# Pre-norm attention and binary feed-forward layer on one core: a transfer queue in another order, masks laid by small matmuls, normalisations with a tensor as third operand

## The chip, the cores and the metric

The kernel runs on one core of a Trainium2 chip. Its program is written out for each engine: PE (TensorE, matrix multiplication into PSUM), DVE (VectorE), ACT (ScalarE), POOL (GpSimd) and SP (SyncE, which here only issues DMA transfers, in order). The engines meet in semaphores. The metric is the time of one launch on the device in microseconds (us).

## The reference

```python
# x: (8, 1024, 256); 16 heads of 16; window 128
def attn(x):
    q = (x @ Wq.T + bq).reshape(B, S, 16, 16)      # k and v alike
    scores = einsum('bqhd,bkhd->bhqk', q, k) * 0.25
    mask = (j <= i) & (j >= i - 128)
    attn = softmax(where(mask, scores, -10000.)) + 1e-9
    return einsum('bhqk,bkhd->bqhd', attn, v).reshape(B, S, 256) @ Wo.T + bo
x = x + attn(layernorm(x))
x = x + einsum('bsi,oi->bso', layernorm(x), sign(weight))
```

## The kernel before

Each of the 8 sequences is cut into 8 tiles of 128 rows, and two tiles make a pair. The program is a software pipeline of slots, one for each of the 64 tiles and four more. In a slot each engine works on stages of different tiles. `parts(b, t)` says which: for slot t, `nm` (turn the negative row maxima of tile t+2 and store them), `mx` (the rough scores of tile t+3 for its row maxima), `pv` (probabilities times values, tile t-1), `xr` (load x of tile t-2 again), `op` (output projection and first residual of tile t-3), `ff` (second layer and store of tile t-4). Stages of a pair run in every other slot: `tqv` (transpose, q and v projections) and `load` (load x) in odd slots; `k` (k projection) and `ln` (first layer norm, two tiles) in even ones. "Odd" and "even" below are the slot's number; slot numbers run on over the sequences, eight to each.

What the change and the prediction touch:

- **The SP queue.** `slot` in the SP program runs through the stages in written order. In an odd slot: the stored maxima (`stack_nmax`, L296), `load_x` (L242), `stack_q` (L252 and L262: it waits for `q_16`, which ACT makes near the end of that slot, then issues 2 + 6 transfers), `load_xr` (L303), and the store of the result (L323). In an even slot: `stack_nmax`, `set_k_max` (L272, after `k_16`), `stack_k` (6 transfers, L288), `load_xr`, the store. SP never passes over an instruction that waits.
- **The residual.** `load_xr` brings x of a tile into `xr`. In the next slot POOL adds the bias row to it (`add_biases`, L428), and after that, in even slots, works out 1/sqrt(variance) of the new pair (`rsqrt1`, L392 and L394). Then it zeroes the masked probabilities with two `affine_select` instructions over 128x1024 (L417 and L420); two more of them open the next slot.
- **The end of an even slot on DVE.** `norm1` writes the normalised pair, two instructions (L652), and only behind them in DVE's order comes x2 = ga + xr (L779). PE opens the next slot with four transposes into the bank `ga` (`turn_u`, L994), which waits for x2, because x2 reads `ga`. `norm2` (L662) is the second layer norm, at the head of the next slot on DVE.
- **Row maxima.** PE makes rough bf16 scores of blocks of 32 queries against 160 keys, in three groups of heads (3, 3 and 2 heads of each half; `max_scores`). Each group first lays the mask into the two PSUM banks (L923; L919 for a sequence's first tile, with all 160 columns instead of the outer 64) and then adds 24 or 16 small products (L931), 16 rows by 32 columns of the array, with row groups 0 and 64 and four column groups. DVE takes the maxima (L695), and only then may PE lay the next group's mask.
- **q_stack.** The exact scores read q with its negative maximum as one more row of the product. The two halves of the heads lie 64 partitions apart, and so `stack_nmax` wrote them by two transfers.

```python
last = v.tensor_scalar(xn[:, j], xs[:, i, j], mv1[:, j, 0:1], rs1[:, j:j + 1], ALU.subtract, ALU.mult)
...
v.tensor_tensor(x2[:, i], ga[:, 0:D], xr[:, i], ALU.add).then_inc(x2_done, 1)
```

## Time and profile before

| | |
|---|---|
| median of the runs | 953.24 us (lowest 949.41) |
| profiled execution, its own time | 948.12 us |
| its span, first to last instruction | 946.4 us |
| mean granted TensorE clock | 0.887 |
| busy: PE, DVE, ACT, POOL | 788.6, 630.9, 487.9, 443.9 us |

The profile is of one execution. Busy time counts any work in flight on an engine; a wait is the idle time of an engine just before an instruction, with what ended it. The granted clock is 1.00 at 2.4 GHz and 0.50 at 1.2 GHz; a stretch with both lies between.

### The profile page before, as it was taken

Reading aid. Unit: us, or ns where it says so; the run is one execution under the profiler, and the core shown is the slowest. Engines: PE = TensorE matmul, PEld = TensorE weight load, DVE = VectorE, ACT = ScalarE, POOL = GpSimd, SP = SyncE. Lnnn points to the kernel's source line nnn. Section 1 sums busy time; section 2 is a strip of 40 time slices with the busy share of each in tenths; the row PEclk is TensorE's granted clock in tenths of the full one; section 3 lists DMA queues with packets and bytes.
Section 4 is the critical chain, followed back from the end, with each engine's and each line's share of the span. In section 5 each row is a group of like instructions: output and inputs, shape, how many; then the busy total and the mean of one; then the engine's idle time right before and its main releaser. Section 6 shows DMA issues by size and latency. Waiting matters only on the chain.

```text
span 946.4 us, 29257 instructions
## 1 busy us (share of the span) xinstructions
PE 788.6 (83%) x11920; PEld 643.7 (68%) x11920; DVE 630.9 (67%) x1171; ACT 487.9 (52%) x1029; POOL 443.9 (47%) x596
## 2 busy tenths in 40 slices
PE   2679898888888988888988888899888899888984
PEld 2467677776677766777776766777666777766763
DVE  6555667676767766776667766667667677666543
ACT  2245665555556554555645555565545565454640
POOL 6324444545535453544445454354444444545551
PEclk9767999889889997989979998988988999887995
DMA  3884656556646555775556677555567645457310
GB/s 94 113 105 84 106 93 97 94 83 114 113 79 106 90 94 88 114 113 85 89 86 102 95 114 109 93 95 83 86 106 113 102 86 87 92 79 108 65 34 22
DMA packets 105077, 87.80 MB, mean 93 GB/s; under 512 B 12336, under 2 KB 104944, under 8 KB 104944
## 3 DMA queue, kind: packets, MB, share of 16 engines
q1 hardware_dynamic: 103008, 84.49, 55.8%
q8 instruction: 95, 1.56, 0.8%
q10 hardware_dynamic: 1936, 1.45, 0.5%
q14 instruction: 38, 0.31, 0.1%
HBM read 18.22 MB, written 8.39 MB: 28 GB/s over the span
## 4 chain that ended last, share of the span: by engine, by line
PE 49%; DMA 15%; SPq 12%; DVE 10%; issue 6%; POOL 6%; ACT 1%; POOLq 0%; DVEq 0%; ACTq 0%
DMA xr<-x 14%; SPq L262 12%; PE sc L965 10%; PE gc L838 10%; PE pv L983 8%; PE ga L838 6%; PE mx L931 4%; DVE xn L652 4%; PE ga L994 2%; POOL rs L394 2%; POOL xr L428 2%; PE gc L853 2%; PE mx L923 2%; PE gb L1023 1%; DVE x L779 1%
## 5 line engine op out<-in xcount | busy, mean ns | idle before, releaser
L537 ACT ACTIVATE prob<-sc 128x512 f32<-128x512 f32 x448 | 264.3, 596 | 216.5 <-PE sc L965 212.6
L965 PE MATMUL sc<-q_stack,k_stack 128*128 128x256 f32 (+1 forms) x1024 | 249.9, 334 | 5.2 <-DMA q_stack<-q_hi 2.5
L965 PEld LDWEIGHTS sc<-q_stack,k_stack 128*128 128x128 f32 x1024 | 171.7, 210 | 53.7 <-issue 45.7
L695 DVE TENSOR_REDUCE nmax<-mx 128x6 f32<-128x960 f32 x188 | 195.1, 1038 | 10.0 <-PE mx L931 5.6
L983 PE MATMUL pv<-prob,v_ones 128*32 128x128 f32 x3840 | 159.0, 297 | 0.0
L420 POOL TENSOR_SCALAR_AFFINE_SELECT prob<-prob 128x1024 f32<-128x1024 f32 x128 | 143.9, 1124 | 5.9 <-ACT prob L539 5.9
L428 POOL TENSOR_TENSOR xr<-xr,brow 128x256 f32<-128x256 f32 x64 | 46.7, 730 | 189.6 <-DMA xr<-x 172.7
L417 POOL TENSOR_SCALAR_AFFINE_SELECT prob<-prob 128x1024 f32<-128x1024 f32 x112 | 122.3, 1092 | 25.1 <-ACT prob L537 25.1
L994 PE MATMUL ga<-ident,u 128*128 128x128 f32 x256 | 45.6, 307 | 89.8 <-DVE x L779 89.6
L983 PEld LDWEIGHTS pv<-prob,v_ones 128*32 128x32 f32 x3840 | 100.2, 116 | 29.5 <-issue 8.6
L433 POOL TENSOR_SCALAR ve<-mv 128x1 f32<-128x1 f32 x64 | 13.9, 217 | 222.0 <-DVE mv L790 222.0
L662 DVE TENSOR_SCALAR xn<-x,mv,rs 128x256 f32<-128x256 f32 x64 | 73.0, 1141 | 63.1 <-POOL rs L435 63.1
L652 DVE TENSOR_SCALAR xn<-xs,mv,rs 128x256 f32<-128x256 f32 x64 | 68.3, 1107 | 47.9 <-POOL rs L394 47.9
L994 PEld LDWEIGHTS ga<-ident,u 128*128 128x128 f32 x256 | 32.1, 156 | 95.4 <-issue 93.1
L931 PE MATMUL mx<-k_max,q_max 16*32 16x160 bf16 x4008 | 77.8, 252 | 0.0
L923 PE MATMUL mx<-window,ident 128*128 128x192 bf16 x330 | 59.5, 267 | 19.2 <-DVE nmax L695 19.2
L675 DVE SCALAR_TENSOR_TENSOR q_lo<-gc,bq,q_hi 128x256 fp32r<-128x256 f32 x64 | 28.0, 480 | 63.0 <-ACT q_hi L488 63.0
L547 ACT ACTIVATE nmax_t<-gb 16x128 fp32r<-16x128 f32 x64 | 16.5, 258 | 102.7 <-PE gb L943 102.7
L931 PEld LDWEIGHTS mx<-k_max,q_max 16*32 16x32 bf16 x4008 | 36.2, 94 | 37.7 <-issue 32.2
L409 POOL TENSOR_TENSOR vsum<-vsum,v_ones 128x256 f32<-128x256 f32 x56 | 41.6, 743 | 21.7 <-ACT v_ones L522 19.2
L539 ACT ACTIVATE prob<-sc 128x256 f32<-128x256 f32 x64 | 24.8, 387 | 47.8 <-PE sc L965 47.6
L683 DVE SCALAR_TENSOR_TENSOR k_lo<-gc,bk,k_hi 128x256 fp32r<-128x256 f32 x60 | 26.3, 480 | 32.3 <-ACT k_hi L499 32.3
(136 smaller groups left out, 1501.8 us busy)
## 6 DMA issues: line engine op xcount, KB each, us to landing
q_stack<-q_hi SPq DMA_DIRECT2D x128, 128.0 KB, 4.6
k_stack<-k_hi SPq DMA_DIRECT2D x128, 128.0 KB
xs<-x SPq DMA_DIRECT2D x32, 256.0 KB, 3.4
q_stack<-q_lo SPq DMA_DIRECT2D x64, 128.0 KB, 4.7
k_stack<-k_lo SPq DMA_DIRECT2D x64, 128.0 KB
xr<-x SPq DMA_DIRECT2D x64, 128.0 KB, 4.9
out<-x SPq DMA_DIRECT2D x64, 128.0 KB, 4.5
q_max<-q SPq DMA_DIRECT2D x64, 64.0 KB
```

The source lines that it names most:

```text
L262: sp.dma_start(q_stack[at:at + DK, :, cols].bitcast(F32), src[:, c, :].bitcast(F32)).then_inc(q_stacked[i], 16)
L417: g.affine_select(out=nxt, in_=nxt, compare_op=ALU.is_ge, fill=0.0, base=0, pattern=[[0, HB], [-1, P]], channel_multiplier=1)
L420: g.affine_select(out=own, in_=own, compare_op=ALU.is_ge, fill=0.0, base=0, pattern=[[0, HB], [1, P]], channel_multiplier=-1).then_inc(pro ...
L537: a.activation(prob[:, own:nxt + 1:nxt - own, 2 * f:2 * f + 2, :], sc, ACT.Exp, scale=SCALE).then_inc(exp_done, 1)
L652: last = v.tensor_scalar(xn[:, j], xs[:, i, j], mv1[:, j, 0:1], rs1[:, j:j + 1], ALU.subtract, ALU.mult)
L695: v.tensor_reduce(nmax[:, n % 2, :].rearrange("p (r h) -> p r h", r=C)[:, :, h0:h0 + m], banks[:, :, 0:WIN * m].rearrange("p r (h k) -> p ...
L838: last = mm(dst, l, r, start=j == 0, stop=j == len(terms) - 1)
L923: mm(dst[:, :, ends, :], ident16[:, :], window[:, hs, :].rearrange("p h (e k) -> p h e k", k=QB)[:, :, ends, :], start=True, stop=False, s ...
L931: last = mm(banks[QB * blk:QB * (blk + 1), rg, WIN * j:WIN * (j + 1)], q_max[64 * rg:64 * rg + DK, h, aq:aq + QB], k_max[64 * rg:64 * rg + ...
L965: last = mm(sc_bank[f % 2][:, 2 * P * j:2 * P * j + q], k_stack[:, h, ak:ak + P], q_stack[:, h % HB, P * t:P * t + q], start=True, stop=True)
L983: last = mm(pv_bank[32 * j:32 * (j + 1), P * cg:P * (cg + 1)], v_ones[:, tile, h, :], prob[:, part, h, :], start=cg == 0 and k == 0, stop= ...
L994: last = nc.tensor.transpose(ga[:, P * cg:P * (cg + 1)], u[:, t % 2, P * cg:P * (cg + 1)], ident[:, :])
```

## The change

Four things are changed.

1. **The order of the SP queue.** `load_xr` comes first in every slot. `stack_k` moves from the even slot into the odd one behind it, right after `load_xr` (`"ks": pair(1)`). The eight transfers that bring q into `q_max` and `q_stack` move from the end of an odd slot into the next, even one, with `set_k_max` between the two halves of `q_stack`.
2. **The maxima** of a tile go by one transfer with 2 partitions as its target, instead of two transfers.
3. **The mask** is laid by eight matmuls of 32 rows by 32 columns of the array for a group (two row groups, four column groups) instead of two over the whole array. The source holds 32 rows of the mask once and is read for every head by an access pattern that repeats it. POOL makes these masks with 10 instructions at the start, instead of 24.
4. **Both normalisations** are `scalar_tensor_tensor` with 1/sqrt(variance) as a tensor read with step 0, in place of `tensor_scalar` with two values per partition.

```diff
             return now, {"nm": tile(2), "mx": tile(3), "pv": tile(-1), "xr": tile(-2), "op": tile(-3), "ff": tile(-4),
-                         "tqv": pair(5), "k": pair(4), "ks": pair(2), "ln": pair(6), "load": pair(7)}
+                         "tqv": pair(5), "k": pair(4), "ks": pair(1), "ln": pair(6), "load": pair(7)}
...
-            def stack_q(b, p):
+
+            def stack_q(b, p, c):
+                i, _ = halves(p)
+                cols = slice(2 * P * p, 2 * P * (p + 1))
+                g = PAIRS * b + p
+
                 wait(sp, sc_filled, SC_FILLS * (TILES * (b - 1) + 2 * p + 2))
                 if g == 0:
                     sp.wait_ge(q_zeroed, 1)
                 sp.wait_ge(q_hi_done, g + 1)
                 sp.wait_ge(q_lo_done, g + 1)
-                for c in range(C):
-                    for r, src in enumerate((q_hi, q_hi, q_lo)):
-                        at = 64 * c + DK * r
-                        sp.dma_start(q_stack[at:at + DK, :, cols].bitcast(F32),
-                                     src[:, c, :].bitcast(F32)).then_inc(q_stacked[i], 16)
+                for r, src in enumerate((q_hi, q_hi, q_lo)):
+                    at = 64 * c + DK * r
+                    sp.dma_start(q_stack[at:at + DK, :, cols].bitcast(F32),
+                                 src[:, c, :].bitcast(F32)).then_inc(q_stacked[i], 16)
...
             def stack_nmax(b, t):
                 i, _ = halves(t)
                 sp.wait_ge(nm_done, TILES * b + t + 1)
-                for c in range(C):
-                    at = 64 * c + 3 * DK
-                    sp.dma_start(q_stack[at:at + 1, :, P * t:P * (t + 1)].bitcast(F32),
-                                 nmax_t[HB * c:HB * (c + 1), i, :].bitcast(F32)).then_inc(nmax_stacked[i], 16)
+                at = 3 * DK
+                sp.dma_start(q_stack[at:at + 65:64, :, P * t:P * (t + 1)].bitcast(F32),
+                             nmax_t[:, i, :].bitcast(F32)).then_inc(nmax_stacked[i], 16)
...
             def slot(b, t):
                 now, part = parts(b, t)
+                if part["xr"]:
+                    load_xr(*part["xr"])
+                if part["ks"]:
+                    stack_k(*part["ks"])
                 if part["nm"]:
                     stack_nmax(*part["nm"])
                 if part["load"]:
                     load_x(*part["load"])
-                if part["tqv"]:
-                    stack_q(*part["tqv"])
                 if part["k"]:
+                    set_q_max(*part["k"])
+                    stack_q(*part["k"], 0)
                     set_k_max(*part["k"])
-                if part["ks"]:
-                    stack_k(*part["ks"])
-                if part["xr"]:
-                    load_xr(*part["xr"])
+                    stack_q(*part["k"], 1)
...
+                for rg in range(C):
+                    rows = slice(64 * rg, 64 * rg + QB)
+                    pool.wait_ge(pool_setup, 3)
+                    g.affine_select(out=edges[rows, 0, :], in_=edges[rows, 0, :], compare_op=ALU.is_ge, fill=MASKED,
+                                    base=0, pattern=[[1, QB]], channel_multiplier=-1).then_inc(windows_done, 1)
+                    g.affine_select(out=edges[rows, 1, :], in_=edges[rows, 1, :], compare_op=ALU.is_ge, fill=MASKED,
+                                    base=0, pattern=[[-1, QB]], channel_multiplier=1).then_inc(windows_done, 1)
+                    m = window0[rows, :, :]
+                    for k, (base, cm, step, per) in enumerate(((0, -1, 1, 0), (P, 1, -1, 0), (-P, 0, 1, QB))):
+                        pool.wait_ge(pool_setup, 3 + 2 * rg + k)
+                        g.affine_select(out=m, in_=m, compare_op=ALU.is_ge, fill=MASKED, base=base,
+                                        pattern=[[per, P // QB], [step, WIN]],
+                                        channel_multiplier=cm).then_inc(pool_setup if k < 2 else windows_done, 1)
+                pool.wait_ge(windows_done, 6)
...
                 for j in range(2):
-                    last = v.tensor_scalar(xn[:, j], xs[:, i, j], mv1[:, j, 0:1], rs1[:, j:j + 1],
-                                           ALU.subtract, ALU.mult)
+                    last = v.scalar_tensor_tensor(xn[:, j], xs[:, i, j], mv1[:, j, 0:1],
+                                                  rs1[:, j:j + 1].broadcast_to([P, D]), ALU.subtract, ALU.mult)
                 last.then_inc(xn_done, 1)
...
                 wait(dve, t2_filled, n)
-                v.tensor_scalar(xn2[:, :], x2[:, i], mv2[:, 0:1], rs2[:, :],
-                                ALU.subtract, ALU.mult).then_inc(xn2_done, 1)
+                v.scalar_tensor_tensor(xn2[:, :], x2[:, i], mv2[:, 0:1], rs2[:, :].broadcast_to([P, D]),
+                                       ALU.subtract, ALU.mult).then_inc(xn2_done, 1)
...
-                hs = slice(0, len(heads))
-                for rg in range(C):
-                    dst = banks[:, rg, 0:WIN * len(heads)].rearrange("p (h e k) -> p h e k", h=len(heads), k=QB)
-                    if t == 0:
-                        mm(dst, ident16[:, :], window0[:, hs, :].rearrange("p h (e k) -> p h e k", k=QB),
-                           start=True, stop=False, skip_group_check=True)
-                    else:
-                        ends = slice(0, WIN // QB, WIN // QB - 1)
-                        mm(dst[:, :, ends, :], ident16[:, :],
-                           window[:, hs, :].rearrange("p h (e k) -> p h e k", k=QB)[:, :, ends, :],
+                m = len(heads)
+                for blk in range(P // QB):
+                    for rg in range(C):
+                        rows = slice(64 * rg, 64 * rg + QB)
+                        dst = banks[QB * blk:QB * (blk + 1), rg, 0:WIN * m].rearrange("p (h e k) -> p h e k", h=m, k=QB)
+                        if t == 0:
+                            mask = window0[rows, blk, :].rearrange("p (e k) -> p e k", k=QB)
+                        else:
+                            mask = edges[rows, :, :]
+                            dst = dst[:, :, 0:WIN // QB:WIN // QB - 1, :]
+                        mm(dst, ident16[rows, rows], mask.unsqueeze(1).broadcast_to(list(dst.shape)),
                            start=True, stop=False, skip_group_check=True)
...
-                        pe.wait_ge(nmax_stacked[i], 32 * (TILES // 2 * b + m + 1))
+                        pe.wait_ge(nmax_stacked[i], 16 * (TILES // 2 * b + m + 1))
```

The SP queue before, in the steady part: an even slot:

```order
L296 DMA q_stack<-nmax_t 1x8x128 x2
L272 DMA k_max<-k 16x8x256 x2
L288 DMA k_stack<-k_hi 16x8x256
L288 DMA k_stack<-k_lo 16x8x256
L288 DMA k_stack<-k_hi 16x8x256 x2
L288 DMA k_stack<-k_lo 16x8x256
L288 DMA k_stack<-k_hi 16x8x256
L303 DMA xr<-x 128x256
L323 DMA out<-x 128x256
```

Here `xr` stands behind eight transfers of k. SP in the odd slot behind it, before:

```order
L296 DMA q_stack<-nmax_t 1x8x128 x2
L242 DMA xs<-x 128x2x256
L252 DMA q_max<-q 16x8x256 x2
L262 DMA q_stack<-q_hi 16x8x256 x2
L262 DMA q_stack<-q_lo 16x8x256
L262 DMA q_stack<-q_hi 16x8x256 x2
L262 DMA q_stack<-q_lo 16x8x256
L303 DMA xr<-x 128x256
L323 DMA out<-x 128x256
```

Here `xr` stands behind eight transfers of q. The SP queue of the changed kernel in the same even slot:

```order
L306 DMA xr<-x 128x256
L299 DMA q_stack<-nmax_t 2x8x128
L251 DMA q_max<-q 16x8x256 x2
L266 DMA q_stack<-q_hi 16x8x256 x2
L266 DMA q_stack<-q_lo 16x8x256
L276 DMA k_max<-k 16x8x256 x2
L266 DMA q_stack<-q_hi 16x8x256 x2
L266 DMA q_stack<-q_lo 16x8x256
L327 DMA out<-x 128x256
```

The q transfers are in this slot now, around those of `k_max`, and `xr` is ahead of all. SP in the odd slot behind it, changed:

```order
L306 DMA xr<-x 128x256
L292 DMA k_stack<-k_hi 16x8x256
L292 DMA k_stack<-k_lo 16x8x256
L292 DMA k_stack<-k_hi 16x8x256 x2
L292 DMA k_stack<-k_lo 16x8x256
L292 DMA k_stack<-k_hi 16x8x256
L299 DMA q_stack<-nmax_t 2x8x128
L242 DMA xs<-x 128x2x256
L327 DMA out<-x 128x256
```

`xr` moved from behind six or eight large transfers to the head, the q transfers left the odd slot, and the k transfers entered it.

PE at the third group of row maxima in a slot, before (`window` is the mask, `ident` the identity):

```order
L965 MATMUL sc<-q_stack,k_stack 128x256 x2
L923 MATMUL mx<-window,ident 128x2x2x32 x2
L931 MATMUL mx<-k_max,q_max 32x160 x16
L983 MATMUL pv<-prob,v_ones 32x128 x16
L965 MATMUL sc<-q_stack,k_stack 128x256 x2
```

and in the changed kernel:

```order
L965 MATMUL sc<-q_stack,k_stack 128x256 x2
L924 MATMUL mx<-edges,ident 32x2x2x32 x8
L931 MATMUL mx<-k_max,q_max 32x160 x16
L983 MATMUL pv<-prob,v_ones 32x128 x16
L965 MATMUL sc<-q_stack,k_stack 128x256 x2
```

Only the mask's matmuls changed, from two over the array to eight of a sixteenth of it; what stands around them is as it was.

## Rows read from the trace of the kernel before

**Rows 1.** Waits, whole span: engine, line, waited for; us, times, longest us.

```profile
POOL xr L428 <- DMA xr<-x: 172.7, 43, 7.2
...
PE ga L994 <- DVE x L779: 89.6, 32, 4.0
```

**Rows 2.** Waits of the SP queue, whole span.

```profile
SPq L250 <- ACT q L505: 267.4, 30, 11.3
```

**Rows 3.** Timeline of SP's issues, slots 27 and 28: start, us, what.

```profile
435.55 0.60 SPq L262 DMA_DIRECT2D q_stack<-q_hi  x1
...
438.17 1.64 SPq L262 DMA_DIRECT2D q_stack<-q_lo  x1
439.85 0.59 SPq L303 DMA_DIRECT2D xr<-x  x1
```

**Rows 4.** Timeline of DVE, POOL and PE, end of even slot 28.

```profile
442.66 0.25 DVE L641 BATCH_NORM_AGGREGATE mv<-st 128x2 f32<-128x6 f32 x2
...
443.46 0.81 DVE L695 TENSOR_REDUCE nmax<-mx 128x4 f32<-128x640 f32 x1
...
444.20 0.74 POOL L428 TENSOR_TENSOR xr<-xr,brow 128x256 f32<-128x256 f32 x1 [5.73 <-DMA xr<-x]
...
444.91 0.23 POOL L392 TENSOR_SCALAR ve<-mv 128x2 f32<-128x2 f32 x1
...
445.22 0.72 POOL L394 TENSOR_TENSOR rs<-ve,half 128x2 f32<-128x2 f32 x1
445.90 1.09 POOL L417 TENSOR_SCALAR_AFFINE_SELECT prob<-prob 128x1024 f32<-128x1024 f32 x1
445.97 2.26 DVE L652 TENSOR_SCALAR xn<-xs,mv,rs 128x256 f32<-128x256 f32 x2 [1.70 <-POOL rs L394]
...
446.94 1.14 POOL L420 TENSOR_SCALAR_AFFINE_SELECT prob<-prob 128x1024 f32<-128x1024 f32 x1
...
448.15 0.41 DVE L779 TENSOR_TENSOR x<-ga,xr 128x256 f32<-128x256 f32 x1
...
448.71 0.63 PE L994 MATMUL ga<-ident,u 128*128 128x128 f32 x4 [3.44 <-DVE x L779]
```

**Rows 5.** Slots by windows: us, busy of PE, PEld, DVE, ACT, POOL; PEclk, DMA, GB/s.

```profile
462.38:476.12 13.74, 9.91 (x184) 8.08 (x182) 10.16 (x19) 7.91 (x17) 7.74 (x10) 1.00 0.79 134
505.32:517.39 12.07, 11.03 (x165) 9.09 (x166) 8.62 (x17) 7.23 (x16) 5.96 (x8) 1.00 0.44 66
726.74:740.08 13.34, 13.34 (x166) 11.04 (x167) 8.78 (x17) 7.46 (x16) 5.97 (x8) 0.77 0.25 45
443.89:452.50 8.61, 5.17 (x63) 3.47 (x62) 5.82 (x10) 2.93 (x6) 6.73 (x9) 0.83 0.95 141
```

**Rows 6.** Timeline of POOL and DVE near slot 3.

```profile
91.86 1.17 POOL L417 TENSOR_SCALAR_AFFINE_SELECT prob<-prob 128x1024 f32<-128x1024 f32 x1 [0.77 <-ACT prob L537]
92.11 1.19 DVE L724 TENSOR_TENSOR cb_lo<-brow,cb_hi 128x256 fp32r<-128x256 f32 x1
```

**Rows 7.** Instructions of line L724: duration ns least/median/most, starts.

```profile
L724 DVE TENSOR_TENSOR cb_lo<-brow,cb_hi x8: 425/426/1189, 92.1 to 866.6; 128x256 fp32r<-128x256 f32 x8
```

**Rows 8.** Timeline of PE, slot 30: two groups of row maxima.

```profile
463.17 0.34 PE L923 MATMUL mx<-window,ident 128*128 128x192 bf16 x2
463.44 0.40 PE L931 MATMUL mx<-k_max,q_max 16*32 16x160 bf16 x24
463.77 0.64 PE L983 MATMUL pv<-prob,v_ones 128*32 128x128 f32 x16
...
469.83 0.33 PE L931 MATMUL mx<-k_max,q_max 16*32 16x160 bf16 x16
470.09 1.08 PE L983 MATMUL pv<-prob,v_ones 128*32 128x128 f32 x32
```

**Rows 9.** Timeline of PE in odd slot 33.

```profile
505.32 0.63 PE L994 MATMUL ga<-ident,u 128*128 128x128 f32 x4 [2.98 <-DVE x L779]
...
509.75 0.34 PE L923 MATMUL mx<-window,ident 128*128 128x192 bf16 x2 [1.01 <-DVE nmax L695]
```

More of the change, by code:

```diff
@@ L327, in _ @@
             load_x(0, 2)
-            stack_q(0, 0)
+            set_q_max(0, 0)
+            for c in range(C):
+                stack_q(0, 0, c)
             set_k_max(0, 0)
@@ L336, in _ @@
             load_x(0, 3)
-            stack_q(0, 1)
+            set_q_max(0, 1)
+            for c in range(C):
+                stack_q(0, 1, c)
             set_k_max(0, 1)
@@ L341, in _ @@
             stack_nmax(0, 1)
-            stack_q(0, 2)
             run(sp, slot)
```

34 lines of the change are left out of this document (7 added, 27 removed).

## The prediction

> **What bounds the kernel now.** I read the waits first, then the queue behind the longest, then one slot boundary instruction by instruction, then the clock. The waits [rows 1] show two that belong together: POOL waits 172.7 us for `xr` to land, and PE waits 89.6 us, 32 times, for x2 (L779) before it may transpose into `ga`. PE is the busiest engine and waits for little else, so the 89.6 us are time of the whole kernel. The queue's own waits [rows 2] say why `xr` is late: SP stands 267.4 us at the head of `stack_q`, waiting for `q_16`. When it comes, SP issues q's transfers, the last of them issued from 438.17 to 439.81, and only then `xr` [rows 3], which lands as POOL's idle time ends, at 444.20. There [rows 4] the reader should follow one line: `xr` lands, POOL adds the bias row (0.74), makes 1/sqrt (0.23 and 0.72) and is done at 445.94; DVE, free since 443.46 + 0.81 = 444.27, has waited 1.70 us for it; two normalisations take 2.26, x2 0.41, and PE starts at 448.71 after 3.44 us of idleness. x2 itself did not wait for `xr`, it stands behind the normalisations. In the steady part I count 27 such boundaries, the ends of the even slots from 4 to 56, each with about 3.3 us; odd slots end without a wait.
>
> The price is more than the wait. An even slot has the full clock (the first of [rows 5]), but the odd slot behind a stall often begins at half clock: of two slots with the same work one has clock 1.00 and takes 12.07 us, the other 0.77 and 13.34 (the second and third of [rows 5]). So a lost clock costs up to 1.27 us in such an odd slot. That the gain is no more is due to DVE: at full clock PE waits 1.01 us in the middle of the odd slot for the first row maxima [rows 9].
>
> **Part 1, the queue.** `xr` is now issued at the head of the slot ahead, some 12 us before POOL wants it. `rsqrt1` then waits only for the statistics: they end at 442.66 + 0.25 = 442.91, and from the start of L392 to the end of L394 it is 445.94 - 444.91 = 1.03 [rows 4], with 0.1 for the signal: done at 444.05. POOL goes on at once with its two selects, 1.85 us earlier than now (445.90). What is late next is DVE, free at 444.27, and then the selects themselves, as part 4 says. With nothing else changed both normalisations would end 1.85 us earlier.
>
> What this moves elsewhere: q's eight transfers go into the even slot, where SP has nothing else after k's six have left it, and `stack_k` into the odd slot. Their needs are a slot and more away (q_stack three slots, k_stack the next slot). The tightest is `k_max`, issued as now at about 8 us into the even slot, between the halves of q_stack. I cost it at nothing, covered by some 3 us up to PE's first group of maxima. The transfers of a pair are the same bytes; I take none for them. One maxima transfer instead of two saves SP an issue of about 0.7 us a slot; SP waits, so it is worth nothing, and the cover is SP's own wait, whose length after the change is the rest of each slot.
>
> **Part 3, the mask.** A group of row maxima now: mask 463.44 - 463.17 = 0.27 us, 24 products 463.77 - 463.44 = 0.33 us; in the third group 16 products take 470.09 - 469.83 = 0.26 [rows 8]. So eight more products of 160 columns cost 0.07 us, and the eight run side by side. By that row eight mask matmuls of 192 columns cost 0.08 us, since the tiled stretch with its fixed part is there already; a group saves 0.27 - 0.08 = 0.19. The other end: all eight in a row, 8 x 0.08 = 0.64, which is 0.37 dearer. I take the first, because it is the same tiling in the same place. In an even slot only the first group counts (0.19: the statistics and the normalisations hang on k, which follows it on PE); the rest goes into the stall. In an odd slot what stands behind the row maxima counts, the second and third group, 0.19 and 0.17, together 0.36.
>
> The Trainium skill, "TensorE: Matmul & The Clock Gate", section "Measured speedup vs the span model", gives a pack of tiles the time of one matmul and about 4 ns for each further tile; by it, as an estimate, the eight masks would take 0.11 us and a group would save 0.16. No row here times such a mask.
>
> **Part 4, the normalisations.** Each takes 1.13 us in the middle of the kernel, in step with the selects of POOL: the first ends behind L417, the pair ends at 448.23, 0.15 after L420 [rows 4]. Does an instruction with two tensors from SBUF escape that? One row shows it does not: `cb_lo<-brow,cb_hi`, two SBUF tensors of 256 elements, took 1.19 us where it met a select [rows 6], while its median over 8 is 0.426 [rows 7]. The select ran 91.86 to 93.03, and the instruction ended at 93.30, 0.27 behind it. The new form reads the row of x and 1/sqrt from SBUF, both, so it will wait as this one did and end 0.27 behind a select instead of 0.14: 0.13 dearer, not cheaper. Of part 1's 1.85 us, 0.25 goes this way and 1.60 is left for an even slot. `norm2` meets the first select of the next slot and costs 0.13 more ahead of the first row maxima. The other end is no wait at all, 0.43 to 0.48 each; that is the first rival.
>
> The skill's page "SBUF — State Buffer", section "Who interferes with whom", says that a DVE instruction with two SBUF inputs contends with a GpSimd instruction that reads SBUF. The row agrees, 1.19 against 0.426 us.
>
> **The sum**, against the profiled execution's 948.1 us. Even slots: 27 x 1.60 = 43, and 27 x 0.19 = 5 of the mask. Odd slots: 0.36 - 0.13 = 0.23, over 28 with a little more in a sequence's first tile: 7. The clock: the stall shrinks from 3.4 to about 2.2 us. Its length alone does not settle the clock: behind the 2.98 us at 505.32 [rows 9] the slot was at 1.00 [rows 5]. I give a third of 27 x 1.27 = 34 back: 11 (bounds 0 and 34). The start, where POOL makes fewer masks, and the end, where slots hang on other chains: 2. Together 68, so 880. The median of the runs is 5 us above the profiled execution, which is less than my error; I predict 881.
>
> **Rivals.**
>
> *The new form does not wait for POOL.* For it: its second tensor is one value read again and again, and no row shows such an operand from SBUF beside another SBUF tensor. Against it: rows 6. It would give 444.27 + 2 x 0.48 + 0.41 + 0.15 = 445.8 for PE's start, 2.9 us earlier than now, and `norm2` 0.7 earlier, which takes most of the 1.01 us wait of rows 9. With the clock up, even slots save 3.1, odd ones about 2.4 (from the clock and those 0.7 us): 27 x 5.5 = 148, so about 800. Chance 0.12.
>
> *Slower: the maxima queue behind k.* In the odd slot `stack_nmax` now stands behind `xr` and six k transfers, and PE's first scores of the next slot wait for it. Those are 7 x 128 KB = 0.9 MB; the burst of k from 443.89 moved 141 GB/s (the fourth of [rows 5]), so they take 6.4 us, and the maxima land near 8.5 us into a slot of 12: 3.5 us to spare. If transfers left over from the even slot pushed that back past the slot's end, each us would cost 28. It gives slower than before from 2.4 us of stall in each odd slot on, that is a landing 6 us later than I reckon; with 3 us it would be 880 + 84 = 964. Chance 0.04.
>
> *The mask's matmuls run one after another.* Then even slots lose 0.37 instead of winning 0.19, and odd ones lose some 0.9: 27 x 0.56 + 28 x 1.1 = 46 more, 926. Chance 0.07. For it is only that the mask's source is read with a repeating pattern; against it rows 8.
>
> *The order alone does little*, because something else holds x2, such as `rsqrt1` behind `sum_v` or the transfers of q now in the even slot: only the masks and a little remain, 930 to 945. Against it: POOL stands idle for 5.73 us ahead of `xr` [rows 4]. Chance 0.05.
>
> **How the numbers follow.** My forecast has 0.72. Its own bounds: the clock gives nothing (891) or all (857), the masks nothing (892 with the clock as taken) and both at their worst 903; DVE and the queue add some 10 on either side, so 845 to 913. For 8 in 10 the range must take half of the dear cases: high 920. At the low side the first rival lies at 800 with its own spread; I reach to 820 and leave most of it out. Measurement tells 2% from no change, which is 19 us: under 934 is faster. Faster: 0.72 + 0.12 + 0.07 less a little = 0.90; same 0.06; slower 0.04.
>
> **What would show it.** In the changed profile: POOL's wait for `xr` gone (under 20 of 172.7 us); SP's longest wait no longer at the head of the q transfers in front of `xr`; L651, the new `norm1`, about 1.2 us each and starting within 0.3 us of a select; PE's wait for x2 about 2.0 to 2.2 us at the end of even slots, in all 55 to 65 us; mask to first product on PE about 0.1 us in place of 0.27; mean clock 0.90 to 0.93; even slots 12.1, odd slots 13.3 on average. If the normalisations take 0.5 us, the first rival holds. If PE's waits for the maxima's transfer (L965 behind `q_stack<-nmax_t`) reach 50 us, the second does. Wrong would be the forecast also if another wait takes the place of x2's at the head of the odd slots, `k_max` above all.

## The result and the profile after

The kernel after takes 898.43 us (median of 5 runs, 892.86 to 922.62) against 953.24 us before (949.28 to 959.47, and one run of 1605.70): ratio 0.941, with an interval of 0.934 to 0.948. The forecast was 881 with a range of 820 to 920. The profiled execution of the kernel after took 922.62 us, the longest of its five, at a mean clock of 0.858, while the other four took 892.86 to 900.28 us at 0.894 to 0.903, so what is read below of the clock and the length of its odd slots holds for that execution, and no other was profiled.

The page: busy time, and the granted clock in 40 slices.

```profile
PE 791.2 (86%) x13072; PEld 661.8 (72%) x13072; DVE 640.9 (70%) x1171; ACT 488.8 (53%) x1029; POOL 454.2 (49%) x582
...
PEclk9868989799889787799978788889978889778995
```

The waits of the kernel after, whole span: engine, line, waited for; us, times, longest us.

```profile
POOL ve L391 <- DVE mv L640: 116.0, 32, 10.8
...
PE ga L994 <- DVE x L778: 52.7, 31, 2.0
...
PE mx L924 <- DVE nmax L694: 23.4, 33, 3.4
...
POOL xr L427 <- DVE brow L727: 17.1, 8, 3.0
```

A wait of POOL for `xr` to land is not in the list any more; its 172.7 us of [rows 1] are gone, and POOL's wait is now the one for the statistics, as it should be. PE's wait for x2 fell from 89.6 to 52.7 us. The waits of SP's queue say what took the place of the 267.4 us of [rows 2] at the head of q's transfers:

```profile
SPq L306 <- DVE x L778: 170.3, 61, 6.5
...
SPq L251 <- ACT q L504: 12.1, 2, 9.0
```

The end of an even slot, from the timelines of POOL, DVE and PE, against [rows 4]:

```profile
426.48 0.74 POOL L427 TENSOR_TENSOR xr<-xr,brow 128x256 f32<-128x256 f32 x1
...
430.46 0.25 DVE L640 BATCH_NORM_AGGREGATE mv<-st 128x2 f32<-128x6 f32 x2
...
430.80 0.23 POOL L391 TENSOR_SCALAR ve<-mv 128x2 f32<-128x2 f32 x1 [3.58 <-DVE mv L640]
431.11 0.73 POOL L393 TENSOR_TENSOR rs<-ve,half 128x2 f32<-128x2 f32 x1
431.26 0.81 DVE L694 TENSOR_REDUCE nmax<-mx 128x4 f32<-128x640 f32 x1
431.80 1.09 POOL L416 TENSOR_SCALAR_AFFINE_SELECT prob<-prob 128x1024 f32<-128x1024 f32 x1
431.99 2.40 DVE L651 SCALAR_TENSOR_TENSOR xn<-xs,mv,rs 128x256 f32<-128x256 f32 x2
432.84 1.28 POOL L419 TENSOR_SCALAR_AFFINE_SELECT prob<-prob 128x1024 f32<-128x1024 f32 x1
434.32 0.41 DVE L778 TENSOR_TENSOR x<-ga,xr 128x256 f32<-128x256 f32 x1
434.88 0.63 PE L994 MATMUL ga<-ident,u 128*128 128x128 f32 x4 [1.96 <-DVE x L778]
```

POOL adds the bias row four us ahead of the statistics and is idle when they end. DVE goes from the row maxima straight into the normalisations, but these take 2.40 us (2.26 before), in step with the two selects: the last select ends at 434.12, the second normalisation at 434.39. The lines of the two forms, duration in ns least/median/most:

```profile
L651 DVE SCALAR_TENSOR_TENSOR xn<-xs,mv,rs x64: 476/1173/1307, 13.8 to 810.1; 128x256 f32<-128x256 f32 x64
...
L661 DVE SCALAR_TENSOR_TENSOR xn<-x,mv,rs x64: 484/1296/1298, 103.5 to 914.8; 128x256 f32<-128x256 f32 x64
```

A group of row maxima on PE, against [rows 8]:

```profile
423.17 0.48 PE L965 MATMUL sc<-q_stack,k_stack 128*128 128x256 f32 x2
423.58 0.27 PE L924 MATMUL mx<-edges,ident 32*32 32x192 bf16 x8
423.67 0.39 PE L931 MATMUL mx<-k_max,q_max 16*32 16x160 bf16 x24
423.99 0.32 PE L983 MATMUL pv<-prob,v_ones 128*32 128x128 f32 x4
```

Four slots in a row by windows, even and odd in turn (us; busy of PE, PEld, DVE, ACT, POOL; PEclk, DMA share, GB/s), against [rows 5]:

```profile
422.70:434.88 12.18, 9.68 (x202) 8.00 (x200) 10.36 (x19) 8.10 (x17) 7.67 (x10) 1.00 0.58 107
434.88:447.99 13.11, 13.11 (x216) 11.10 (x217) 8.97 (x17) 7.46 (x16) 6.32 (x9) 0.87 0.65 108
447.99:460.16 12.17, 9.60 (x202) 7.99 (x200) 10.35 (x19) 7.88 (x17) 8.00 (x10) 1.00 0.52 102
460.16:475.66 15.50, 15.50 (x215) 13.40 (x216) 9.00 (x17) 5.99 (x16) 5.25 (x8) 0.67 0.57 94
```

The even slots are close to the forecast (12.1 on average). These odd slots are full of PE work from end to end, at a lower clock: that is where the forecast and this execution part. From the starts of the first `ga<-ident,u` of each slot I worked out the mean over the 27 even slots 4 to 56 and the 27 odd ones 5 to 57, for each kernel of this study. "Stall" is PE's idle time at the end of the even slots. "At half" is the time that TensorE spends at 1.2 GHz in place of 2.4 GHz, 2 x (1 - mean clock) x span.

| kernel | median us | ratio (interval) | even slot / stall | odd slot / clock | at half, us |
|---|---|---|---|---|---|
| before | 953.24 | | 13.83 / 3.20 | 13.92 / 0.82 | 214 |
| after | 898.43 | 0.941 (0.934 to 0.948) | 12.17 / 1.88 | 14.64 / 0.76 | 262 |
| e1_scalar | 866.70 | 0.911 (0.904 to 0.919) | 11.89 / 1.61 | 13.05 / 0.93 | 114 |
| e2_wide_mask | 898.52 | 0.945 (0.937 to 0.953) | 12.26 / 1.74 | 13.88 / 0.89 | 144 |
| e3_queue_only | 869.56 | 0.915 (0.910 to 0.921) | 11.99 / 1.48 | 12.99 / 0.98 | 73 |
| e4_no_select | 798.45 (one run) | | 10.66 / 0.38 | 11.96 / 1.00 | 54 |
| e5_fill | 873.05 | 0.921 (0.917 to 0.924) | 12.16 / 0.58 | 13.07 / 0.97 | 72 |
| e6_x2_first | 860.12 | 0.906 (0.902 to 0.910) | 10.43 / 0.15 | 14.09 / 0.93 | 126 |
| e8_select_early | 832.89 | 0.878 (0.873 to 0.883) | 10.66 / 0.38 | 12.96 / 0.98 | 64 |
| e9_all | 789.98 | 0.832 (0.829 to 0.836) | 10.55 / 0.27 | 11.87 / 1.00 | 50 |
| e10_three_op | 797.16 | 0.838 (0.835 to 0.842) | 10.67 / 0.38 | 11.92 / 1.00 | 51 |
| e11_all_wide_mask | 803.42 | 0.845 (0.841 to 0.849) | 10.69 / 0.17 | 12.16 / 1.00 | 50 |
| e12_all_x2_first | 790.84 | 0.833 (0.828 to 0.837) | 10.43 / 0.15 | 11.97 / 1.00 | 49 |
| e13_old_queue | 987.37 | 1.039 (1.033 to 1.044) | 14.55 / 4.22 | 14.38 / 0.76 | 302 |

So the profiled execution gained 27 x 1.66 = 45 us in the even slots, lost 27 x 0.72 = 19 in the odd ones, and the rest of the span came out even: 946.4 - 920.8 = 25.6. Some 50 to 70 us of every figure under "at half" lie ahead of slot 4 and behind slot 57 (70 before, 68 after): e9, with all its slots between at 1.00, keeps 50.

### The profile page after: what moved, and what is told of

Its sections match the earlier page's. It is cut to its first block, busy times and chain, and to the rows that moved or that the text cites. A ratio compares the mean times of both kernels' runs of the same rounds, so it can differ in the third digit from the quotient of the medians.

```text
span 920.8 us, 31506 instructions
## 1 busy us (share of the span) xinstructions
PE 791.2 (86%) x13072; PEld 661.8 (72%) x13072; DVE 640.9 (70%) x1171; ACT 488.8 (53%) x1029; POOL 454.2 (49%) x582
## 4 chain that ended last, share of the span: by engine, by line
PE 62%; DVE 25%; issue 6%; ACT 2%; POOL 2%; SPq 2%; DMA 1%; DVEq 0%; POOLq 0%; ACTq 0%
PE gc L837 15%; PE sc L965 13%; PE pv L983 10%; PE ga L837 7%; DVE xn L651 6%; DVE nmax L694 5%; PE ga L994 3%; PE mx L924 3%; PE mx L931 3%; PE gb L1023 2%; DVE st L635 2%; PE gc L852 2%; DVE xn L661 2%; DVE k_lo L682 2%; ACT k_hi L498 2%
## 5 line engine op out<-in xcount | busy, mean ns | idle before, releaser
L965 PE MATMUL sc<-q_stack,k_stack 128*128 128x256 f32 (+1 forms) x1024 | 254.4, 340 | 2.9 <-DMA k_stack<-k_hi 2.2
L965 PEld LDWEIGHTS sc<-q_stack,k_stack 128*128 128x128 f32 x1024 | 176.3, 217 | 51.9 <-issue 42.6
L419 POOL TENSOR_SCALAR_AFFINE_SELECT prob<-prob 128x1024 f32<-128x1024 f32 x128 | 155.0, 1211 | 8.4 <-ACT prob L538 8.4
L416 POOL TENSOR_SCALAR_AFFINE_SELECT prob<-prob 128x1024 f32<-128x1024 f32 x112 | 122.8, 1097 | 30.3 <-ACT prob L536 30.3
L661 DVE SCALAR_TENSOR_TENSOR xn<-x,mv,rs 128x256 f32<-128x256 f32 x64 | 81.4, 1272 | 63.4 <-POOL rs L434 63.4
L994 PE MATMUL ga<-ident,u 128*128 128x128 f32 x256 | 44.7, 303 | 53.0 <-DVE x L778 52.7
L931 PE MATMUL mx<-k_max,q_max 16*32 16x160 bf16 x4008 | 79.7, 257 | 0.0
L651 DVE SCALAR_TENSOR_TENSOR xn<-xs,mv,rs 128x256 f32<-128x256 f32 x64 | 72.3, 1168 | 3.2 <-POOL rs L393 3.2
L391 POOL TENSOR_SCALAR ve<-mv 128x2 f32<-128x2 f32 x32 | 7.3, 229 | 116.0 <-DVE mv L640 116.0
L924 PE MATMUL mx<-edges,ident 32*32 32x192 bf16 (+1 forms) x1320 | 46.9, 261 | 20.1 <-DVE nmax L694 20.0
L924 PEld LDWEIGHTS mx<-edges,ident 32*32 32x32 bf16 x1320 | 18.6, 89 | 46.4 <-DVE nmax L694 27.9
L931 PEld LDWEIGHTS mx<-k_max,q_max 16*32 16x32 bf16 x4008 | 49.8, 101 | 3.0 <-issue 2.5
```

Of the source, the lines that this page charges most:

```text
L416: g.affine_select(out=nxt, in_=nxt, compare_op=ALU.is_ge, fill=0.0, base=0, pattern=[[0, HB], [-1, P]], channel_multiplier=1)
L419: g.affine_select(out=own, in_=own, compare_op=ALU.is_ge, fill=0.0, base=0, pattern=[[0, HB], [1, P]], channel_multiplier=-1).then_inc(pro ...
L651: last = v.scalar_tensor_tensor(xn[:, j], xs[:, i, j], mv1[:, j, 0:1], rs1[:, j:j + 1].broadcast_to([P, D]), ALU.subtract, ALU.mult)
L661: v.scalar_tensor_tensor(xn2[:, :], x2[:, i], mv2[:, 0:1], rs2[:, :].broadcast_to([P, D]), ALU.subtract, ALU.mult).then_inc(xn2_done, 1)
L924: mm(dst, ident16[rows, rows], mask.unsqueeze(1).broadcast_to(list(dst.shape)), start=True, stop=False, skip_group_check=True)
L931: last = mm(banks[QB * blk:QB * (blk + 1), rg, WIN * j:WIN * (j + 1)], q_max[64 * rg:64 * rg + DK, h, aq:aq + QB], k_max[64 * rg:64 * rg + ...
```

## The experiments

All are edits of the kernel after, and ratios are to the kernel before, run on the same chip. The kernel after itself was not run again beside them. Differences from its 898.43 us therefore compare runs on different chips; by the ratios they are some 4 to 6 us smaller (28 in place of 32 for e1_scalar, 19 in place of 25 for e5_fill).

**The three-operand form undone.** The theory: the form costs 0.13 us an instruction, plus what it takes from the clock. Its rival: it costs nothing measurable, and the low clock comes from the order of the transfers or the masks.

```diff
-  last = v.scalar_tensor_tensor(xn[:, j], xs[:, i, j], mv1[:, j, 0:1],
-                                rs1[:, j:j + 1].broadcast_to([P, D]), ALU.subtract, ALU.mult)
+  last = v.tensor_scalar(xn[:, j], xs[:, i, j], mv1[:, j, 0:1], rs1[:, j:j + 1],
+                         ALU.subtract, ALU.mult)
```

(and the same for `xn2`.)

> Undoes part 4 alone: both normalisations are tensor_scalar again, the rest is the changed kernel. Theory (the port): either form waits for POOL's select, and the three-operand form then ends 0.13 us later. So norm1 goes from 2.40 to about 2.26 us, norm2 from 1.30 to 1.16, even slots from 12.17 to about 11.95, and the kernel from 898 to 885 to 895. Rival (the new form is the gain): the time goes up from 898 by 10 us or more, since POOL would be held back by the old form. Rival (no effect): within 3 us of 898.

866.70 us, 32 faster than after, and 18 below the range that was expected. The lines of e1, to be set beside those of after:

```profile
L651 DVE TENSOR_SCALAR xn<-xs,mv,rs x64: 403/1040/1175, 13.8 to 760.2; 128x256 f32<-128x256 f32 x64
...
L661 DVE TENSOR_SCALAR xn<-x,mv,rs x64: 412/1164/1167, 100.7 to 859.8; 128x256 f32<-128x256 f32 x64
```

Each instruction is 0.13 us shorter (1.173 to 1.040, 1.296 to 1.164), the even slot 0.28. That is 27 x 0.28 = 8 us of the 32. In an odd slot `norm2` counts as well: at the full clock slot 29 takes 12.66 us here and 12.82 in e5_fill, which has the three-operand form, and the other odd slots differ by 0.11 to 0.15, so 27 x 0.13 = 4 us more. The form's own duration costs 11 to 12 us. The windows of e1, an even slot and two odd ones:

```profile
399.00:410.89 11.89, 9.66 (x201) 7.99 (x200) 9.94 (x19) 8.09 (x17) 7.37 (x10) 1.00 0.53 100
410.89:423.55 12.66, 11.64 (x215) 9.99 (x216) 8.70 (x17) 7.24 (x16) 6.17 (x9) 1.00 0.72 118
...
435.45:449.56 14.11, 14.07 (x216) 12.14 (x217) 8.83 (x17) 5.90 (x16) 5.12 (x8) 0.76 0.66 104
```

The second slot has the full clock and takes 12.66; the third has 0.76 and takes 14.11, where the same place of another sequence (slot 23 of e1) takes 12.36 at 1.00. In the profiled execution of after only 3 of the 27 odd slots had the full clock, in e1 17. So 0.27 us more stall goes with the other 20 us, lost to the clock in the odd slots (17 by the ratios).

**The masks undone.** 128x128 matmuls with `window` as before; all else as after.

```diff
-  for blk in range(P // QB):
-      for rg in range(C):
...
-          mm(dst, ident16[rows, rows], mask.unsqueeze(1).broadcast_to(list(dst.shape)),
+  for rg in range(C):
...
+          mm(dst[:, :, ends, :], ident16[:, :],
+             window[:, hs, :].rearrange("p h (e k) -> p h e k", k=QB)[:, :, ends, :],
```

> Undoes part 3 alone: the mask is laid by two matmuls over the whole array again. Theory (the masks run side by side, but the switch of the array from whole to tiled now stands ahead of them, so a group saves 0.10 us and not 0.19): even slots 12.17 to about 12.27, odd slots 0.2 to 0.3 us longer at full clock and more at half clock; 903 to 912. Rival (masks worth the full 0.19 and 0.36 that I had reckoned): 910 to 920. Rival (masks worth nothing, they are hidden by DVE): 895 to 901.

898.52 against 898.43, as the rival without effect had it: the masks won no time in the kernel after. That is not because they save nothing. The same odd slot (27) at the full clock, first in after and then with the wide masks:

```profile
408.93:422.70 13.77, 12.49 (x221) 10.59 (x222) 10.28 (x22) 7.36 (x16) 6.31 (x9) 1.00 0.63 108
```

```profile
402.10:416.13 14.03, 12.84 (x203) 10.73 (x204) 10.28 (x22) 7.35 (x16) 6.30 (x9) 1.00 0.53 99
```

The small masks save 0.26 us there and 0.09 in an even slot (12.26 against 12.17), some 9 us in 27 of each. The clock takes them back: the four runs of e2 had a mean of 0.920 to 0.937, the four faster ones of after 0.894 to 0.903. Why the clock is higher with the wide masks is not shown.

**Both undone**, so that the queue and the one maxima transfer are left.

```diff
-  mm(dst, ident16[rows, rows], mask.unsqueeze(1).broadcast_to(list(dst.shape)),
+  mm(dst[:, :, ends, :], ident16[:, :],
...
-  last = v.scalar_tensor_tensor(xn[:, j], xs[:, i, j], mv1[:, j, 0:1],
+  last = v.tensor_scalar(xn[:, j], xs[:, i, j], mv1[:, j, 0:1], rs1[:, j:j + 1],
```

> Of the change only the SP queue's order and the one maxima transfer stay; masks and normalisations are those of before. Theory (the queue is nearly the whole gain): even slots fall from 13.8 to about 12.0 us, 27 of them, so about 49 us less than the 953 of before, plus or minus what the clock does in the odd slots (bounds 10): 895 to 912. Rival (the parts add up only together, the queue alone is followed by another wait at x2): above 925.

869.56 us, where 895 to 912 was expected: the queue alone is worth more than the whole change. Its even slots fell by 13.83 - 11.99 = 1.84, which is the 1.85 that part 1 reckoned for unchanged normalisations, and its odd slots by 0.93, with a clock of 0.98. Against e1 the masks win 3 us here, inside the intervals. The stall is the shorter one in e3, 1.48 against 1.61: what a mask gives back ahead of the normalisations is waited for at their end.

The same two odd slots (29 and 31) of e3, to be set beside those of after: both at the full clock.

```profile
415.52:428.63 13.11, 12.30 (x197) 9.96 (x198) 8.79 (x17) 7.24 (x16) 6.17 (x9) 1.00 0.69 115
440.63:453.25 12.62, 11.54 (x197) 9.81 (x198) 8.71 (x17) 5.78 (x16) 5.06 (x8) 1.00 0.60 113
```

**No selects.** Does the wait of the new form come from the selects at all? Of POOL's two selects of a half one is taken out and the other cut to one element, so this kernel leaves out the zeroing of masked probabilities and its output is another.

```diff
-  if t < TILES - 1:
-      nxt = prob[:, 2 + n % 3, HB * r:HB * (r + 1), :]
-      g.affine_select(out=nxt, in_=nxt, compare_op=ALU.is_ge, fill=0.0, base=0,
-                      pattern=[[0, HB], [-1, P]], channel_multiplier=1)
-  own = prob[:, n % 2, HB * r:HB * (r + 1), :]
+  own = prob[:, n % 2, HB * r:HB * r + 1, 0:1]
```

> Leaves out the zeroing of masked probabilities: POOL's two selects over 128x1024 become one over one element (the output is that of unmasked probabilities). Otherwise the changed kernel. Theory (the port): with no select beside them the normalisations take 0.43 to 0.48 us each instead of 1.17 to 1.30, x2 comes 1.4 us earlier, PE's wait for x2 at the end of even slots falls from 1.96 to under 0.6 us, and the time is 800 to 840. Rival (the form costs 1.2 us by itself in this place): the normalisations stay above 1 us and the time stays within 10 us of 898.

798.45 us in one run. The normalisations take their own time, 477 and 485 ns at the median, and the stall is 0.38 us. That is the time of the prediction's first rival, reached for another reason: not the form was spared by the selects, the selects were gone. It relieves POOL of the selects as a whole too; the experiment with the selects moved, below, keeps that work.

**The stall filled.** If the odd slots are slow only because TensorE stood idle before them, then work of no use in the stall must bring the clock back. 14 matmuls of 256 columns are put there in most even slots; their result is not used.

```diff
+  if k and now and t != 2:
+      pe.wait_ge(k_lo_done, PAIRS * k[0] + k[1] + 1)
+      for _ in range(14):
+          mm(gc[:, 0:2 * P], w_hi["q"][:, 0, 0:P], w_hi["q"][:, 1, :], start=True, stop=True)
```

> The changed kernel, with 14 matmuls of 256 columns of constant weights put into PE's stall at the end of the even slots with t = 0, 4 and 6 (their results are not used; they go to the bank gc behind the last read of k's bank by DVE). 14 take about 1.65 us, less than the stall of 1.96, so nothing is made later by them. Theory (the odd slots are long because of the clock, and the clock is lost by idleness at the end of the even slot): the odd slots with t = 1, 5 and 7 run at clock 1.00 and take 11.9, 12.7 and 12.4 us, as they do in the kernel with the scalar form; even slots stay at 12.2; 855 to 872 in place of 898. Rival (the clock goes by the whole load of PE, or the half-clock slots do not matter): clock and time as in the changed kernel, 890 or more.

873.05 us, 25 faster than after, by doing more work; its four runs had a mean clock of 0.959 to 0.963, against 0.894 to 0.903. The even slots kept their length (12.16 against 12.17), the odd ones have 13.07 (14.64 in the slowest execution of after). PE's timeline in e5 shows the filling in the stall, and the windows two odd slots:

```profile
438.32 1.83 PE L1129 MATMUL gc<-wh_q 128*128 128x256 f32 x14
...
440.66 0.63 PE L994 MATMUL ga<-ident,u 128*128 128x128 f32 x4 [0.35 <-DVE x L778]
```

```profile
415.68:428.50 12.82, 11.80 (x216) 10.01 (x217) 8.84 (x17) 7.59 (x17) 6.32 (x9) 1.00 0.70 114
440.66:453.15 12.49, 11.27 (x215) 9.69 (x216) 8.81 (x17) 5.94 (x17) 5.19 (x8) 1.00 0.60 117
```

The same transfers, masks and form as after, and the full clock in most slots: the idleness in the stall took it. It is not the whole of it, since slots 15, 25, 39 and 49, behind filled stalls, still had 0.87 or 0.88. The form's 32 us in the first experiment come apart as 11 to 12 for its own duration and about 20 by way of the clock, and that is the size of what the filling brings.

**x2 ahead of the normalisations.** DVE makes x2 and its statistics first, then `norm1`.

```diff
-  if part["ln"]:
-      norm1(*part["ln"])
   if part["op"]:
       ...
       v.bn_aggr(mv2[:, :], st2[:, :]).then_inc(mv2_done, 1)
+  if part["ln"]:
+      norm1(*part["ln"])
```

> The changed kernel, with x2 and its statistics ahead of norm1 in DVE's order, so that PE's wait for x2 no longer contains the two normalisations. Theory (the stall is norm1's time ahead of x2, and the clock hangs on the stall): even slots fall to about 10.6 us without a wait at their end; norm1 then runs in the first 2.6 us of the odd slot, and x transposed (t1) and norm2 come later there, 0.5 to 1.5 us lost again in the odd slots; clock above 0.97; 820 to 850. Rival (it only moves the wait): the odd slots grow by the 2.4 us that the even ones lose, 870 or more.

860.12 us, 10 above the range expected. The stall is gone (even slots 10.43), but the odd slots are longer than in e3, 14.09 against 12.99: `norm1` now takes DVE's time there, and PE's wait moved to the row maxima, 45.6 us where it was 23.4. The odd slots' clock is 0.93, so it does not hang on the stall at the end of the even slots alone.

```profile
PE mx L924 <- DVE nmax L694: 45.6, 54, 3.5
```

**The selects of the tile ahead of `rsqrt1`.** POOL does them while it waits for the statistics anyway.

```diff
-  if part["ln"]:
-      rsqrt1(*part["ln"])
   if now:
       mask_probs(*now, 0)
+  if part["ln"]:
+      rsqrt1(*part["ln"])
```

> The changed kernel, with POOL's order changed: the two selects of the slot's own tile go ahead of rsqrt1 instead of behind it, into the 3.6 us in which POOL waits for the statistics. Theory (norm1 is long only because POOL's selects run beside it): norm1 takes 0.48 us an instruction, x2 comes 1.4 us earlier, the wait at the end of even slots falls from 1.96 to about 0.6 us, even slots to 10.8, the clock of the odd slots rises to 0.97 or more and they take 12.9 on average; 27 x (1.4 + 1.5) = 78 off 898: 815 to 835. Rival (the form costs its time anyway): within 5 us of 898.

832.89 us, 66 faster than after by an exchange of two calls. The medians of the two lines:

```profile
L651 DVE SCALAR_TENSOR_TENSOR xn<-xs,mv,rs x64: 472/476/1356, 13.8 to 722.6; 128x256 f32<-128x256 f32 x64
...
L661 DVE SCALAR_TENSOR_TENSOR xn<-x,mv,rs x64: 483/1295/1299, 98.2 to 820.6; 128x256 f32<-128x256 f32 x64
```

`norm1` no longer meets a select, 476 ns in place of 1173; `norm2`, whose selects were not moved, still does.

**All together.** tensor_scalar, the selects ahead of `rsqrt1`, and POOL waits for `xn2` before the selects that `norm2` used to meet; queue and masks as after.

```diff
   now, part = parts(b, t)
+  if part["ff"]:
+      bb, tt = part["ff"]
+      pool.wait_ge(xn2_done, TILES * bb + tt + 1)
```

> The best guess from all theories: the changed kernel with tensor_scalar, the selects ahead of rsqrt1, and POOL waiting for norm2 before it begins the selects of the next slot, so that neither normalisation meets a select. Theory: norm1 and norm2 take 0.41 us each, even slots 10.6 to 10.8, and odd slots lose PE's wait for the first row maxima (0.7 of it), 12.2 on average: 785 to 805. Rival (POOL's new wait holds up the masked probabilities that PE needs): even slots as expected but PE waits for POOL in the middle of slots, over 815.

789.98 us, ratio 0.832, the fastest kernel of this study. Its waits and two slots:

```profile
POOL prob L416 <- DVE xn L664: 27.7, 53, 0.5
...
PE ga L997 <- DVE x L781: 8.3, 25, 0.6
```

```profile
368.29:378.79 10.50, 9.67 (x202) 8.00 (x200) 7.89 (x19) 7.50 (x16) 7.32 (x10) 1.00 0.55 102
378.79:390.69 11.90, 11.64 (x215) 9.99 (x216) 8.04 (x17) 7.85 (x18) 6.13 (x9) 1.00 0.83 140
```

The added wait costs POOL 27.7 us in 0.5 us pieces, and POOL has that time. PE is busy for 21.31 of 22.40 us. The end of an even slot in e9's timeline: both selects are over at 419.22, the two normalisations take 0.73 us.

```profile
417.08 1.09 POOL L416 TENSOR_SCALAR_AFFINE_SELECT prob<-prob 128x1024 f32<-128x1024 f32 x1
418.13 1.09 POOL L419 TENSOR_SCALAR_AFFINE_SELECT prob<-prob 128x1024 f32<-128x1024 f32 x1
...
422.10 0.73 DVE L654 TENSOR_SCALAR xn<-xs,mv,rs 128x256 f32<-128x256 f32 x2
```

**The form and the masks in that kernel**, where the clock is up everywhere. The first is e9 with the three-operand form, the second e9 with the wide masks, the third e9 with x2 ahead of `norm1` (the edits shown above).

```diff
-  v.tensor_scalar(xn2[:, :], x2[:, i], mv2[:, 0:1], rs2[:, :],
-                  ALU.subtract, ALU.mult).then_inc(xn2_done, 1)
+  v.scalar_tensor_tensor(xn2[:, :], x2[:, i], mv2[:, 0:1], rs2[:, :].broadcast_to([P, D]),
+                         ALU.subtract, ALU.mult).then_inc(xn2_done, 1)
```

> The kernel of the last call's best guess (selects kept away from both normalisations), but with the three-operand form. Theory (the form itself costs only 0.07 us an instruction; nearly all of its price in the changed kernel came from waiting for the select and then from the clock): even slots 0.2 us longer, odd ones 0.1, 27 of each: 790 + 8 = 798, clock unchanged at 0.97. Rival (the form holds POOL back even without a select in the way): above 805.

> The best guess with the mask laid by two matmuls over the whole array. Theory (a group saves 0.10 us on PE, as in the changed kernel): even slots 0.1, odd ones 0.2 to 0.3 us longer: 790 + 9 = 799. Rival (DVE sets the slots, PE's saving is hidden): 788 to 792.

> The best guess with x2 and its statistics ahead of norm1. Only 0.27 us of PE's wait at the end of even slots is left to win, 27 x 0.27 = 7; norm1's 0.85 us then stands in the next slot, before norm2's input is ready anyway (DVE waits 0.98 us for POOL there), so it should cost little. Theory: 783 to 788. Rival (norm1 late makes the transposes of the new pair late): 795 or more.

797.16, 803.42 and 790.84 us; 798, 799 and 783 to 788 were expected. With no select beside it the new form is 0.07 us longer (e10 against e9):

```profile
L654 DVE SCALAR_TENSOR_TENSOR xn<-xs,mv,rs x64: 469/476/1356, 13.8 to 696.9; 128x256 f32<-128x256 f32 x64
...
L664 DVE SCALAR_TENSOR_TENSOR xn<-x,mv,rs x64: 483/484/486, 99.6 to 787.2; 128x256 f32<-128x256 f32 x64
```

```profile
L654 DVE TENSOR_SCALAR xn<-xs,mv,rs x64: 400/406/1310, 13.8 to 692.1; 128x256 f32<-128x256 f32 x64
...
L664 DVE TENSOR_SCALAR xn<-x,mv,rs x64: 410/413/417, 99.1 to 782.0; 128x256 f32<-128x256 f32 x64
```

It costs 7 us there and 32 in the kernel after. The masks are the other way round: nothing in the kernel after, 13 us here (an even slot 0.14, an odd one 0.29). PE is busy for nearly the whole of both slots, and the clock is 1.00 with either mask and has nothing to take back. Moving x2 ahead wins nothing more.

**The old order of the queue**, all else as after. The q transfers go back into the odd slot and `stack_k` into the even one too. The theory: the queue's order is the whole gain, and without it the other parts are worth little or cost.

```diff
-  if part["xr"]:
-      load_xr(*part["xr"])
-  if part["ks"]:
-      stack_k(*part["ks"])
...
+  if part["ks"]:
+      stack_k(*part["ks"])
+  if part["xr"]:
+      load_xr(*part["xr"])
```

> The changed kernel without part 1: the SP queue has its old order again (one maxima transfer, tiled masks and three-operand normalisations stay). Theory (only the queue pays; the form costs 0.13 us an instruction and the masks give a little): 948 to 965, no faster than before. Rival (masks and form have a gain of their own that the queue's hides): under 940.

987.37 us, 4% slower than before, and 22 above the range expected. The two waits of the kernel before are back, and so is the wait of SP's queue at the head of the q transfers (303.4 us):

```profile
POOL xr L431 <- DMA xr<-x: 166.3, 29, 7.8
...
PE ga L998 <- DVE x L782: 116.3, 32, 5.7
```

Its even slots are 0.72 us longer than before. Means over the 27 say where: the bias row is added 9.78 us into the slot in place of 9.33, though `xr` is issued 0.06 earlier, and the two normalisations take 2.52 in place of 2.26. The second, 0.26, is the form. Why the bias row comes 0.5 us later after the issue of `xr` I did not settle; no run was made for it. The odd slots are longer too, 14.38 at 0.76 against 13.92 at 0.82.

## Why the prediction came out as it did

The direction, the chain that carries it and its place were right; the time was 17 us too low. The sum was 68 us off the profiled 948; the median of after lies 50 below that 948, so 18 are missing: 3 in the even slots (45 of 48), 2 at the start and the end, and, as an estimate, 13 in the odd ones. That last figure comes from the profiled execution, whose odd slots lost 19 where 18 of gain were forecast, 37 short, and from the 24 us by which it lies above the median, if those lie in its odd slots, which no profile shows. The prediction also took 5 us for nothing, by which the median of before lies above its profiled execution; carried along, they would have given 885. The largest term of the miss is the clock's.

*The queue.* Right: with the old form the even slots fell by 1.84 us (e3) where 1.85 was reckoned; with the new one 0.28 of it went again (e1 against after) where 0.25 was. The step "what is late next is DVE, and then the selects" is what the timeline of after shows. e13 shows the other side: without the queue the remaining parts cost 37 us (987 against 950, the median of before in the same runs).

*The selects beside the new form.* Right. The forecast of 1.2 us each held (1.173 at the median), so did the start within 0.3 us of a select (431.99 behind 431.80), and the first rival, that the form escapes the selects, fell. `norm2` at 1.296 beside selects and 0.484 without is the same statement in one line. The Trainium skill, page "SBUF — State Buffer", section "Who interferes with whom", says that a DVE instruction with two SBUF inputs contends with a GpSimd instruction that reads SBUF; these rows agree that the new form waits. They do not show that its repeated second input is the reason, since tensor_scalar, with one tensor from SBUF, waits beside a select too (1.04 us against 0.41 alone). What the new form adds there is the 0.13 us that were forecast.

*PE's wait for x2.* Forecast 2.0 to 2.2 us and 55 to 65 in all; measured 1.88 and 52.7. The prediction started from 3.4 us at one boundary, where the mean of the 27 is 3.20.

*The masks.* The step "a group saves 0.27 - 0.08 = 0.19" was half right. From the mask's start to the first product it fell from 0.27 to 0.09 as reckoned, but from the scores ahead of it to the mask it rose: 463.17 - 462.85 = 0.32 in the kernel before, 423.58 - 423.17 = 0.41 after. From the scores to the work behind the group it is 0.92 and 0.82, so 0.10 is saved. The fixed part of the tiled stretch was not there already, it was moved from behind the mask to ahead of it. The Trainium skill, page "TensorEngine Tiling (Array Packing)", section "Key Properties", says that a change of the tiling mode drains TensorE; both rows fit that, with the change now one step earlier. For the masks 5 us were booked in the even slots and 28 x 0.36 = 10 in the odd ones; at the full clock they are worth 27 x 0.09 = 2 and 27 x 0.26 = 7 (e2 against after), and in the time of after nothing, as the clock took them back. The bounds without the masks hold a slip: 880 + 5 + 10 is 895 and not 892, and with the clock at its worst 906 and not 903.

*The clock.* This is the term that was mis-sized: "I give a third of 27 x 1.27 = 34 back: 11 (bounds 0 and 34)". The third was a guess. With masks and form at what they are worth at the full clock (7 - 4 us), the 13 us missing in the odd slots leave 1 or 2 us of the 11 in the median execution, an estimate with the condition named above. The four faster executions had a mean clock of 0.894 to 0.903, at the lower end of the forecast 0.90 to 0.93. The profiled execution had its odd slots at 0.76 where they were at 0.82, and they took 14.64 us where 13.3 was forecast. What could be had is shown by e3: with the queue alone the odd slots are at 0.98 and 0.93 us shorter, 27 x 0.93 = 25 us. So the 34 in all was not far off, and what the prediction lacked is that the new form would keep most of it away.

The price of one lost clock was too small. I took 1.27 us from two slots at 1.00 and 0.77; in the same trace slots 7 and 31, at the same place of their sequences, are 2.9 apart:

```profile
144.31:157.15 12.84, 12.84 (x198) 11.07 (x198) 8.80 (x17) 5.79 (x16) 5.14 (x8) 0.87 0.39 64
476.12:491.87 15.75, 15.75 (x198) 13.33 (x198) 8.98 (x17) 5.94 (x16) 5.14 (x8) 0.67 0.35 56
```

*The form* follows from that. I priced it at 0.25 us in an even slot and 0.13 in an odd one, some 10 us, and its own duration costs 11 to 12; about 20 more come by the clock, which the prediction put at nothing: with the form kept and the stall filled (e5) the time is 873, 6 above that of e1. Without the form the change would have taken 867, below the forecast. That 881 lies within 2% of the result therefore owes something to luck: the clock's part of it depended on a few tenths of a us that the guess did not look at.

*The other rivals.* The second, the maxima behind k, fell: all waits for their transfer at L965 are 1.2 us. No wait for `k_max` is in the list. The third fell with the 0.09 us from mask to product, the fourth with POOL's wait for `xr`.

*What stays open.* The mean stall and the clock of the odd slots do not line up over all kernels: 3.20 us of stall went with 0.82 before, 1.88 with 0.76 in after, 1.74 with 0.89 in e2, 1.61 with 0.93 in e1, 1.48 with 0.98 in e3, 4.22 with 0.76 in e13. That filling the idleness brings the clock back is shown by e5. What else decides it is not: in e5 the odd slots behind the six stalls left unfilled, about 1.58 us each, had 1.00 four times and 0.89 twice, e6 has 0.15 and 0.93, and e2 and after differ in their masks and in the clock of all their runs.

## What to carry to other kernels

Where the busiest engine is TensorE and it stalls regularly, a stall has two prices, its own length and the clock of the work behind it, and the second can be the larger: here 0.28 us of DVE work in 27 even slots and 0.13 in 27 odd ones cost 11 to 12 us directly and about 20 by the clock. Before looking for a faster form of an instruction, look at what runs beside it: a normalisation took 1.04 to 1.30 us in either form beside a select and 0.41 to 0.48 alone, and moving the selects into POOL's idle time was worth 66 us where the form cost 7. And a transfer that waits for nothing should not stand in a queue behind one that does.

## What was not expected of the hardware

- Matmuls of no use make the kernel faster: 14 whose result nobody reads, 1.83 us in each of most even slots, brought the mean clock from 0.90 to 0.96 and the time from 898 to 873 us.
- Slots of the same work differ by up to a fifth by the clock: in the kernel before the odd slots 7 and 31, with the same count of matmuls and PE busy throughout, took 12.84 us at 0.87 and 15.75 at 0.67.
- The three-operand form with a repeated operand takes 0.07 us more than tensor_scalar where nothing stands beside it (0.476 against 0.406), and 0.13 more where a select does.
- Making the mask small too gained 0.18 us behind it and lost 0.09 ahead of it: the fixed cost of going over to small tiles moved with the place where they begin.
